# Five casts of wd, not three, between the last evacuation of gate and the search of blocks 1 to 3

## Chip, cores and metric

The kernel runs on one core of one Trainium2 chip. The metric is the device time of one launch in microseconds (us), lower is better. It is compared as the median of several runs; one more execution was taken with the hardware profiler, and all times inside the kernel are from that one.

## What is computed

The reference, for 2048 tokens x of width H = 1024, in float32, with I = 2752:

```python
s = silu(x @ w_gate.T)                       # 2048 x 2752
# in each row the I//2 entries of smallest |s| are set to 0
s = where_not_among_the_I//2_smallest_abs(s) * (x @ w_up.T)
x = layernorm(x + s @ w_down.T)
# second part: a feed forward layer with tiled quarter weights and rank-2 additions
g = silu(lin(x, w1q, a1, b1)) * lin(x, w3q, a3, b3)
x = layernorm(x + lin(g, w2q, a2, b2))       # lin = x @ tile(w,4).T + 0.5 * x @ A.T @ B.T
```

The change is in the first part: gate, the selection of the small entries, up and down (weights w_gate, w_up, w_down, in the kernel wg, wu, wd).

## The kernel before

The tokens are worked in four blocks of 512 (b = 0 to 3), each as four tiles t of 128 tokens. A matrix product in float32 precision is made of three passes of TensorE: each operand is split in a high part (a cast to fp32r) and a low part (the difference to the original), and `three` (lines 1405 to 1409) adds high x high, high x low and low x high.

**Pieces of weights.** All three weight matrices go through one ring of RING = 5 places in SBUF. A piece is 128 rows of the contraction by up to 512 columns, 256 KB. For each piece, in the same order everywhere:

- SyncE (SP) waits until TensorE has finished the piece five before it, whose place it takes (`load`, line 396, semaphore pe_used), and issues the load (line 398).
- ScalarE (ACT) casts it to its high part wh (`high_ring`, line 681).
- GpSimd (POOL) makes the low part wl (line 574).
- TensorE (PE) multiplies it with four tiles of tokens (lines 1407 to 1409): 12 matmuls of 512 columns for a piece.

Each engine does its pieces strictly in the order of the program. The order of TensorE is gate(0), up(0), and then for b = 1 to 3: gate(b) (48 pieces of wg), down(b-1) (44 pieces of wd, d = 0 to 43, called d0 to d43 here), up(b) (48 pieces of wu); at the end down(3). So the product with wd of a block runs between gate and up of the next one. The pieces d14 and d15 belong to the half-filled last chunk of rows; they take 8 matmuls, not 12 (lines 1498 and 1499).

**The search.** While TensorE is in down(b-1), VectorE (DVE) and ScalarE look for the threshold of each token of block b, in six rounds (called round 1 to 6). In a round VectorE writes a trial threshold (`negt`, line 969, semaphore probe) and counts the entries below it for tiles 0 and 1 (line 975, two passes); ScalarE counts for tiles 2 and 3 with four Sign activations (line 728), then raises the semaphore signs (line 735), for which VectorE waits (line 978) before it works out the next trial. Since ScalarE must go on casting weights, its search calls `piece()`, the cast of the next piece of wd, behind the first three Sign activations of each round, and 1 or 2 times more behind the round (line 824). A cast whose piece has not landed holds the Sign activation behind it.

After round 6 VectorE picks the exact threshold for the four tiles (lines 1021 to 1038); in front of the last pass of it, it takes the banks of PSUM with the sums of down(b-1), n = 0 (`take_down`, line 1125). The first matmuls of up(b) overwrite these banks and wait for that (line 1472, semaphore d_evac), tile by tile.

**Loads besides the weights.** Right behind the load of d28 SyncE issues the load of y, 2 MB of x in token order (lines 463 and 464), on the same queue.

Of the kernel before, what the change touches and what calls it, by code (L numbers as in the profile page):

```python
# [42 lines left out]
RING = 5  # L43
# [10 lines left out]
ND = 2 * NC  # L54
# [60 lines left out]
def down_at(b):  # L115
    return gate_at(b + 1) + (NG if b < NB - 1 else 0)
# [60 lines left out]
def program(nc, xT, xtok, wg, wu, wd, w13, w2, a13, a2, b1, b3, b2, out):  # L177
    x1 = nc.dram_tensor("x1", (NB, P, NT, H), F32, kind="Internal").ap()
    turning = nc.dram_tensor("turning", (NB, NJ, P, NT * CW), F32, kind="Internal").ap()
    with ExitStack() as ctx:  # L180
# [494 lines left out]
        def _(act):  # L675
# [7 lines left out]
            def high_ring(n, cols):  # L683
                high(raw_in[n % RING], 16 * (n // RING + 1), wh[:, ring(n, cols)], w_in_place[:, ring(n, cols)])
# [4 lines left out]
            def high_d(b, d):  # L689
                high_ring(down_at(b) + d, CW)  # L690
# [5 lines left out]
            def evac(b, j):  # L696

                for t in range(NT):
                    if t < NT - 1:
                        act.wait_ge(g_done, 3 * NJ * b + 3 * j + t + 1)  # L700
                    else:
                        act.wait_ge(pe_used, gate_at(b) + KH * (j + 1))
                    if b == 1:

                        act.wait_ge(u_freed, 8 + 4 * j + t + 1)
                    dst = s0[:, in_chunk(j, t)] if b == 0 else v[:, t, cols(j)]
                    nc.scalar.activation(dst, banks[2 * t + j % 2][:, 0:width(j)], ACT.Silu).then_inc(g_freed, 1)  # L707
# [13 lines left out]
            def search(b, piece, behind):  # L721

                for r in range(ROUNDS):
                    act.wait_ge(probe, ROUNDS * b + r + 1)
                    for t in (2, 3):
                        for h in range(2):
                            st.done()
                            ins = nc.scalar.activation(junka[:, :], v[:, t, h * (I // 2):(h + 1) * (I // 2)], ACT.Sign,  # L728
                                                       bias=negt[:, t:t + 1], accum_out=ssum[:, t - 2, h:h + 1])
                            st.mark(ins)  # L730
                            if t == 2 or h == 0:
                                piece()
                    st.done()

                    act.sem_inc(signs, 1)
                    for _ in range(behind[r]):
                        piece()

            def turned(b, n):

                for j, g in cast_at(b, n):
                    if g == 0:
                        act.wait_ge(t_in[j % 2], 16 * GROUPS * (NJ // 2 * b + j // 2 + 1))
                    nc.scalar.copy(h_part(hTh, j, g), h_part(landed, j, g)).then_inc(t_hi, 1)  # L744

            def up(b):

                for j in range(NJ):
                    for i in range(KH):
                        high_gu(up_at(b), KH * j + i)  # L750
                        turned(b, KH * j + i)
                    if j == 1:
                        norm(b - 1)
# [45 lines left out]
            ahead = iter(range(RING, NG))  # L799
# [16 lines left out]
            def down_then_up(b):  # L816

                for d in range(3):
                    high_d(b - 1, d)
                    if b == 1:  # L820
                        turned(0, NG + d)
                evac(b, NJ - 1)
                ahead = iter(range(3, ND))
                search(b, lambda: high_d(b - 1, next(ahead)), (1, 2, 2, 1, 1, 1))
                for d in ahead:
                    high_d(b - 1, d)
                up(b)

            gate_1()
            down_then_up(1)  # L830
            for b in range(2, NB):
                gate(b)
                down_then_up(b)
# [902 lines left out]
```

## Time and profile before

| | |
|---|---|
| time, median of 3 runs | 1923.15 us (1918.4 to 1924.95) |
| the profiled execution | 1917.84 us, span 1916.0 us |
| TensorE clock granted, mean | 0.999 of full |
| TensorE busy | 1886.9 us, 98% of the span |
| VectorE busy | 1338.0 us, 70% |
| ScalarE busy | 732.6 us, 38% |
| GpSimd busy | 935.7 us, 49% |

The span is from the first to the last instruction; 1.84 us lie around it. A row of the trace such as `378.14 0.50 PE L1407 ...` has the start in us from the beginning of the span, the duration in us, the engine, the line of the kernel and what is written from what; in brackets stands how long the engine was idle before it and who released it. Busy shares of TensorE come from pipelined matmuls with modelled ends, so starts are what is read below.

### The profile page before, as it was taken

How to read it: one execution, taken by the hardware profiler on the slowest of the kernel's cores; microseconds unless marked ns; L12 is line 12 of the kernel's file. 1: busy time of each engine (PE TensorE's matmuls, PEld its weight loads, DVE VectorE, ACT ScalarE, POOL GpSimd, SP SyncE). 2: the span in 40 equal slices, each digit the busy share in tenths (PEclk: the TensorE clock that was granted, in tenths of full speed). 3: DMA queues.
4: the chain of work that ended last, by engine and by line, in shares of the span. 5: the costliest groups of instructions: out<-in, count | busy, mean ns of one | idle time of the engine just before them, and what ended most of it. 6: DMA issues, size and time to landing. Idle time of an engine off the chain costs nothing. (4 is left out here: it accounts for less than half of the span.)

```text
span 1916.0 us, 24248 instructions
## 1 busy us (share of the span) xinstructions
PE 1886.9 (98%) x8952; PEld 1574.7 (82%) x8952; DVE 1338.0 (70%) x1958; ACT 732.6 (38%) x1192; POOL 935.7 (49%) x705
## 2 busy tenths in 40 slices
PE   9999999999999999999999999999999999999998
PEld 7898878888888898887878988889888777887776
DVE  2138898889877437897852489888218998469963
ACT  4347434563234336523243463233242332123312
POOL 5456895455556544555484455555581331013410
PEclk9999999999999999999999999999999999999999
DMA  4333348634478433436763334377742132212212
GB/s 148 91 102 95 99 148 229 177 100 139 125 227 246 114 87 103 145 98 213 192 199 95 96 101 138 121 237 208 221 145 77 57 117 91 88 43 70 97 44 88
DMA packets 119393, 249.78 MB, mean 130 GB/s; under 512 B 13412, under 2 KB 33892, under 8 KB 115920
## 3 DMA queue, kind: packets, MB, share of 16 engines
q1 hardware_dynamic: 114664, 231.43, 40.0%
q10 hardware_dynamic: 4608, 16.78, 2.2%
q8 instruction: 71, 1.16, 0.3%
q14 instruction: 50, 0.41, 0.1%
HBM read 208.31 MB, written 39.85 MB: 130 GB/s over the span
## 5 line engine op out<-in xcount | busy, mean ns | idle before, releaser
L574 POOL TENSOR_TENSOR wl<-w_in_place,wh 128x512 fp32r<-128x512 f32 (+2 forms) x552 | 736.9, 1342 | 600.0 <-ACT wh L681 598.5
L681 ACT CAST wh<-w_in_place 128x512 fp32r<-128x512 f32 (+2 forms) x560 | 328.3, 588 | 728.5 <-DMA w_in_place<-in_wg 283.1
L1407 PE MATMUL banks<-wh,xTh 128*128 128x512 f32 (+2 forms) x1536 | 566.2, 369 | 12.6 <-POOL wl L574 12.4
L1408 PE MATMUL banks<-wl,xTh 128*128 128x512 f32 (+2 forms) x1536 | 563.3, 367 | 0.0
L1409 PE MATMUL banks<-wh,xTl 128*128 128x512 f32 (+2 forms) x1536 | 563.2, 367 | 0.0
L1407 PEld LDWEIGHTS banks<-wh,xTh 128*128 128x128 f32 x1536 | 288.3, 188 | 61.7 <-POOL wl L574 21.7
L1409 PEld LDWEIGHTS banks<-wh,xTl 128*128 128x128 f32 x1536 | 288.3, 188 | 40.1
L1408 PEld LDWEIGHTS banks<-wl,xTh 128*128 128x128 f32 x1536 | 288.4, 188 | 39.6
L1407 PE MATMUL banks<-wh,hTh 128*128 128x512 f32 x672 | 262.2, 390 | 3.1 <-POOL wl L574 3.0
L1408 PE MATMUL banks<-wl,hTh 128*128 128x512 f32 x672 | 261.5, 389 | 0.0
L1409 PE MATMUL banks<-wh,hTl 128*128 128x512 f32 x672 | 261.5, 389 | 0.0
L728 ACT ACTIVATE junka<-v,negt 128x1376 int8<-128x1376 f32 x96 | 138.3, 1441 | 77.8 <-DVE negt L969 77.8
L1407 PEld LDWEIGHTS banks<-wh,hTh 128*128 128x128 f32 x672 | 126.1, 188 | 31.4 <-POOL wl L574 5.4
L975 DVE TENSOR_SCALAR_CACHE_REDUCE junkd<-v,tc 128x2752 int8<-128x2752 f32 x48 | 147.6, 3075 | 0.9
L1409 PEld LDWEIGHTS banks<-wh,hTl 128*128 128x128 f32 x672 | 126.1, 188 | 26.3
L1332 DVE SCALAR_TENSOR_TENSOR acc<-h,a2raw,acc 128x512 f32<-128x512 f32 (+1 forms) x168 | 146.5, 912 | 1.6
L1408 PEld LDWEIGHTS banks<-wl,hTh 128*128 128x128 f32 x672 | 126.1, 188 | 25.8
L1407 PE MATMUL banks<-xsh,w13h 128*128 128x512 f32 (+1 forms) x352 | 142.5, 405 | 0.0
L961 DVE TENSOR_SCALAR sgn<-v 128x512 int8<-128x512 f32 (+2 forms) x72 | 45.0, 625 | 138.6 <-ACT v L707 138.6
L1408 PE MATMUL banks<-xsl,w13h 128*128 128x512 f32 (+1 forms) x352 | 137.6, 391 | 0.0
L1409 PE MATMUL banks<-xsh,w13l 128*128 128x512 f32 (+1 forms) x352 | 137.4, 390 | 0.0
L1205 DVE TENSOR_TENSOR hTl<-landed,hTh 128x512 fp32r<-128x512 f32 (+1 forms) x96 | 104.9, 1136 | 45.4 <-ACT hTh L744 45.3
(143 smaller groups left out, 2176.1 us busy)
## 6 DMA issues: line engine op xcount, KB each, us to landing
w_in_place<-in_wd SPq DMA_DIRECT2D x176, 256.0 KB, 2.8
w_in_place<-in_wg SPq DMA_DIRECT2D x128, 256.0 KB, 2.7
w_in_place<-in_wu SPq DMA_DIRECT2D x128, 256.0 KB, 2.6
turning<-squares SPq DMA_DIRECT2D x16, 1024.0 KB, 4.9
landed<-turning SPq DMA_DIRECT2D x64, 256.0 KB, 5.5
w_in_place<-in_w SPq DMA_DIRECT2D x54, 256.0 KB, 2.9
x_in_place<-in_xT SPq DMA_DIRECT2D x32, 256.0 KB, 5.1
y<-in_xtok SPq DMA_DIRECT2D x4, 2048.0 KB, 7.8
```

The costliest lines, as they stand in the source:

```text
L574: nc.gpsimd.tensor_tensor(lo, landed, hi.bitcast(F32), ALU.subtract).then_inc(done, 1)
L681: nc.scalar.copy(hi, piece).then_inc(hi_done, 1)
L728: ins = nc.scalar.activation(junka[:, :], v[:, t, h * (I // 2):(h + 1) * (I // 2)], ACT.Sign, bias=negt[:, t:t + 1], accum_out=ssum[:, t - ...
L961: step(V.tensor_scalar(sgn[:, t, cols(j)], s, 0.0, 2.0, ALU.is_ge, ALU.mult))
L975: step(V.tensor_scalar(junkd[:, :], v[:, t, :], tc[:, 0, t:t + 1], None, ALU.is_lt, ALU.add, accum_out=tc[:, 1, t:t + 1]))
L1205: V.tensor_tensor(h_part(hTl, j, g), h_part(landed, j, g), h_part(hTh, j, g).bitcast(F32), ALU.subtract).then_inc(t_lo, 1)
L1332: step(V.scalar_tensor_tensor(out=part, in0=h2[0:rows, i, :], scalar=w, in1=part, op0=ALU.mult, op1=ALU.add))
L1407: nc.tensor.matmul(dst, ah, bh, start=start, stop=False)
L1408: nc.tensor.matmul(dst, ah, bl, start=False, stop=False)
L1409: return nc.tensor.matmul(dst, al, bh, start=False, stop=stop)
```

## The change

```diff
@@ down_then_up(b) of ScalarE, line 816
                 evac(b, NJ - 1)
-                ahead = iter(range(3, ND))
+                for d in range(3, RING):
+                    high_d(b - 1, d)
+                ahead = iter(range(RING, ND))
                 search(b, lambda: high_d(b - 1, next(ahead)), (1, 2, 2, 1, 1, 1))
                 for d in ahead:
                     high_d(b - 1, d)
```

Before, ScalarE cast d0, d1 and d2, evacuated the last chunk of gate and entered the search; d3 was cast behind the first Sign activation. Now d3 and d4 are cast before the search, and each place in the search has a piece two later than it had. The number of casts in the search stays 26. What the other engines do, and in which order, is unchanged.

ScalarE where the search of block 1 begins. Names: v is what the search counts in, banks are PSUM, wh is the high part of a piece and w_in_place the landed piece; raw_in0 to raw_in4 are the semaphores of the five places of the ring (d3 waits for raw_in2, d4 for raw_in3). Before:

```order
L707 ACTIVATE v<-banks 128x320 [waits u_freed,pe_used]
L728 ACTIVATE junka,ssum<-v,negt 128x1376 [waits act_s,probe]
L681 CAST wh<-w_in_place 128x512 [waits raw_in2]
L728 ACTIVATE junka,ssum<-v,negt 128x1376 [waits act_s]
L681 CAST wh<-w_in_place 128x512 [waits raw_in3]
```

Now, in the same place:

```order
L707 ACTIVATE v<-banks 128x320 [waits u_freed,pe_used]
L681 CAST wh<-w_in_place 128x512 [waits raw_in2]
L681 CAST wh<-w_in_place 128x512 [waits raw_in3]
L728 ACTIVATE junka,ssum<-v,negt 128x1376 [waits act_s,probe]
L681 CAST wh<-w_in_place 128x512 [waits raw_in4]
```

The casts of d3 (raw_in2) and d4 (raw_in3) moved ahead of the first Sign activation, and d5 (raw_in4) follows it.

ScalarE in round 6, the last, of the search of block 1; the row that waits for probe begins the round. Before, with d25 (raw_in4), d26, d27 between the Sign activations and d28 (raw_in2), d29 (raw_in3) behind them:

```order
L728 ACTIVATE junka,ssum<-v,negt 128x1376 [waits act_s,probe]
L681 CAST wh<-w_in_place 128x512 [waits raw_in4]
L728 ACTIVATE junka,ssum<-v,negt 128x1376 [waits act_s]
L681 CAST wh<-w_in_place 128x512 [waits raw_in0]
L728 ACTIVATE junka,ssum<-v,negt 128x1376 [waits act_s]
L681 CAST wh<-w_in_place 128x512 [waits raw_in1]
L728 ACTIVATE junka,ssum<-v,negt 128x1376 [waits act_s]
L681 CAST wh<-w_in_place 128x512 [waits act_s,raw_in2]
L681 CAST wh<-w_in_place 128x512 [waits raw_in3]
```

Now, with d27 (raw_in1), d28, d29 (raw_in3) between them and d30 (raw_in4) behind:

```order
L728 ACTIVATE junka,ssum<-v,negt 128x1376 [waits act_s,probe]
L681 CAST wh<-w_in_place 128x512 [waits raw_in1]
L728 ACTIVATE junka,ssum<-v,negt 128x1376 [waits act_s]
L681 CAST wh<-w_in_place 128x512 [waits raw_in2]
L728 ACTIVATE junka,ssum<-v,negt 128x1376 [waits act_s]
L681 CAST wh<-w_in_place 128x512 [waits raw_in3]
L728 ACTIVATE junka,ssum<-v,negt 128x1376 [waits act_s]
L681 CAST wh<-w_in_place 128x512 [waits act_s,raw_in4]
```

The cast of d29 moved from behind the round to a place ahead of its fourth Sign activation.

## Rows read from the trace of the kernel before

**Rows 1.** The page, part 1: busy time of each engine.

```profile
PE 1886.9 (98%) x8952; PEld 1574.7 (82%) x8952; DVE 1338.0 (70%) x1958; ACT 732.6 (38%) x1192; POOL 935.7 (49%) x705
```

**Rows 2.** Groups by line, TensorE: busy us, mean ns, idle before, releaser.

```profile
L1407 PE MATMUL banks<-wh,hTh 128*128 128x512 f32 x672 | 262.2, 390 | 3.1 <-POOL wl L574 3.0
```

**Rows 3.** Timeline, block 1, first matmul of d3 on TensorE.

```profile
378.14 0.50 PE L1407 MATMUL banks<-wh,hTh 128*128 128x512 f32 x1 [2.11 <-POOL wl L574]
```

**Rows 4.** Timelines of ScalarE and GpSimd, block 1, round 1: first Sign, d3.

```profile
374.70 1.44 ACT L728 ACTIVATE junka<-v,negt 128x1376 int8<-128x1376 f32 x1 [4.84 <-DVE negt L969]
376.14 0.60 ACT L681 CAST wh<-w_in_place 128x512 fp32r<-128x512 f32 x1
...
376.82 1.27 POOL L574 TENSOR_TENSOR wl<-w_in_place,wh 128x512 fp32r<-128x512 f32 x1 [6.39 <-ACT wh L681]
```

**Rows 5.** Timeline of SyncE, block 1: issues of d7, d28, y and d29.

```profile
376.13 0.33 SPq L398 DMA_DIRECT2D w_in_place<-in_wd  x1
...
434.06 0.33 SPq L398 DMA_DIRECT2D w_in_place<-in_wd  x1
434.50 0.37 SPq L455 DMA_DIRECT2D y<-in_xtok  x1
...
436.78 0.33 SPq L398 DMA_DIRECT2D w_in_place<-in_wd  x1
```

**Rows 6.** The same, block 2 and then block 3: d7 and d29 of each.

```profile
734.98 0.33 SPq L398 DMA_DIRECT2D w_in_place<-in_wd  x1
...
793.89 0.33 SPq L398 DMA_DIRECT2D w_in_place<-in_wd  x1
...
1096.42 0.33 SPq L398 DMA_DIRECT2D w_in_place<-in_wd  x1
...
1155.61 0.33 SPq L398 DMA_DIRECT2D w_in_place<-in_wd  x1
```

**Rows 7.** One tile's view, loads of wd in 366 to 434 us.

```profile
DMA to landing us min/median/max: 2.6/2.7/3.0
```

**Rows 8.** DMA issues, KB and us to landing: y of block 1; d29 of blocks 1, 2, 3.

```profile
y<-in_xtok SPq DMA_DIRECT2D x1, 2048.0 KB, 7.9
...
w_in_place<-in_wd SPq DMA_DIRECT2D x1, 256.0 KB, 6.3
...
w_in_place<-in_wd SPq DMA_DIRECT2D x1, 256.0 KB, 6.1
...
w_in_place<-in_wd SPq DMA_DIRECT2D x1, 256.0 KB, 7.0
```

**Rows 9.** One tile's view, all six loads of y in the kernel.

```profile
DMA to landing us min/median/max: 7.6/8.3/9.7
```

**Rows 10.** Waits of VectorE, 370 to 440 us: total, times, longest.

```profile
DVE sadd L979 <- ACTq L735: 8.7, 6, 1.5
```

**Rows 11.** Timeline of ScalarE: fourth Sign of round 6, blocks 1, 2, 3.

```profile
437.89 1.44 ACT L728 ACTIVATE junka<-v,negt 128x1376 int8<-128x1376 f32 x1
...
795.00 1.44 ACT L728 ACTIVATE junka<-v,negt 128x1376 int8<-128x1376 f32 x1
...
1156.73 1.44 ACT L728 ACTIVATE junka<-v,negt 128x1376 int8<-128x1376 f32 x1
```

**Rows 12.** Timeline of VectorE: take_down, n = 0, blocks 1, 2, 3.

```profile
485.18 2.48 DVE L1125 TENSOR_TENSOR y<-banks,y 128x512 f32<-128x512 f32 x4
...
842.02 2.48 DVE L1125 TENSOR_TENSOR y<-banks,y 128x512 f32<-128x512 f32 x4
...
1202.58 2.63 DVE L1125 TENSOR_TENSOR y<-banks,y 128x512 f32<-128x512 f32 x4 [1.49 <-PE banks L1409]
```

**Rows 13.** Groups by line, VectorE: take_down in the whole kernel.

```profile
L1125 DVE TENSOR_TENSOR y<-banks,y 128x512 f32<-128x512 f32 x32 | 20.3, 681 | 33.7 <-PE banks L1409 33.6
```

**Rows 14.** Timeline of TensorE: first matmul of up(1), up(2), up(3).

```profile
488.20 0.39 PE L1407 MATMUL banks<-wh,xTh 128*128 128x512 f32 x1
...
845.31 0.39 PE L1407 MATMUL banks<-wh,xTh 128*128 128x512 f32 x1
...
1207.03 0.39 PE L1407 MATMUL banks<-wh,xTh 128*128 128x512 f32 x1
```

## The prediction

> **What bounds the kernel now.** I read the page first: TensorE is busy for 98% of the span [rows 1], at a granted clock of 0.999, which is its upper level of 2.4 GHz, in every slice. So only what starts or stops TensorE can move the time, and the change touches ScalarE alone. Next I read the groups by line, for what TensorE waits for inside down: over 672 first matmuls of the pieces of wd it waited 3.0 us in all, for the low parts that GpSimd makes [rows 2]. The timeline shows where most of it lies: 2.11 us at d3 of block 1 [rows 3]. The chain behind it is in the timelines of ScalarE and GpSimd [rows 4]: ScalarE had been idle for 4.84 us, waiting for the first trial threshold, ran the first Sign at 374.70, cast d3 only at 376.14, GpSimd took 1.27 us from 376.82, and TensorE started 0.05 us behind its end. This is what the change removes. The reader is to see also that ScalarE was idle in front of that Sign, so that casts there cost nothing.
>
> Then I followed the search itself, because two pieces more are now cast inside its timed part, and it ends in something that TensorE waits for. In each of the six rounds VectorE waits for ScalarE's signs, 8.7 us in all and 1.5 at the longest [rows 10]. So ScalarE is the slower half of every round, and a delay of a Sign goes straight into the length of the search.
>
> **The gain on TensorE.** Every load waits for the end of the piece five before it, so the issues on SyncE show TensorE's pace: d28 to d29 is 2.72 us [rows 5], 12 matmuls of 0.227. From the issue of d7 to that of d29 are 22 steps; undisturbed they take 22 x 2.72 = 59.84 us, less 2 x 0.91 for d14 and d15 with 8 matmuls each, that is 58.02. The rows say 60.65 in block 1 [rows 5], 58.91 and 59.19 in blocks 2 and 3 [rows 6]. The excess, 2.63, 0.89 and 1.17 us, is all that TensorE lost in this stretch, 4.69 us together. It is more than the 3.0 of the groups, because a stop also costs a slower first matmul and the small stops are not all listed; I take the issues. I credit it in full, since d3 and d4 will be cast in the idle stretch: d7 was issued at 376.13, so d4, three pieces earlier, at about 368, and with the usual 2.7 us [rows 7] it landed near 371, well before 374.70 [rows 4]. In blocks 2 and 3 the first trial comes a little earlier against the loads, but by the same counting back d4 lands near 729.5 and 1091.0, some 2 us ahead of it (an estimate), so the start of the search is not delayed (a small delay would be swallowed below anyway).
>
> **The cost in the search.** Every place in the search now casts a piece that lands two pieces, 5.4 us, later. A piece can be cast no sooner than 2.7 us behind the end of the piece five before it. Counting landings by 2.72 us against the places of the casts, I find the places in rounds 1 to 5 just met, or missed by under 1 us, at most about 2 us in sum in one block (an estimate). In round 6 it is otherwise. There the third cast, ahead of the fourth Sign, is now d29. d29 is the piece issued behind the 2 MB load of y [rows 5], and it took 6.3, 6.1 and 7.0 us to land in the three blocks [rows 8], not 2.7. y took 7.9 us from 434.50, thus to 442.4, and d29 landed at 436.78 + 6.3 = 443.1, right behind it. Before, d29 was cast after the search, where this harmed nobody. Its landing is a point in time, so what the earlier rounds lose is swallowed by it and not added.
>
> The Trainium skill, page "DMA: Bandwidth & Descriptors", section "Queues, rings and completion order", says that on each DMA engine the descriptors of a queue are consumed in ring order, though a later one may finish its write first. The rows agree in that d29 did not overtake y; by the second half of the sentence it could, and the sum would then be that of the first rival below.
>
> The fourth Sign of round 6 starts, at the earliest, 0.60 us (the cast, [rows 4]) behind the landing. With TensorE and so the loads earlier by the gain:
>
> Block 1: 436.78 - 2.63 + 6.3 + 0.6 = 441.05, against 437.89 [rows 11]: 3.16 us later.
> Block 2: 793.89 - 0.89 + 6.1 + 0.6 = 799.70, against 795.00: 4.70 us later.
> Block 3: 1155.61 - 1.17 + 7.0 + 0.6 = 1162.04, against 1156.73: 5.31 us later.
>
> **What waits for the search.** Behind the last signs VectorE has an unbroken stretch of picking up to take_down, which it reached at 485.18, 842.02 and 1202.58 - 1.49 = 1201.09 [rows 12]. In blocks 1 and 2 it did not idle there: TensorE had finished the banks already. The first tile of take_down takes 0.68 us [rows 13], and TensorE can follow 0.05 us behind as it did behind GpSimd (together 0.73). TensorE began up at 488.20, 845.31 and 1207.03 [rows 14]; so the cover over VectorE's chain was 488.20 - 485.91 = 2.29, 2.56 and 5.21 us. That is the cover that hides the change's cost, and the gain on TensorE eats it too. New starts of up:
>
> Block 1: TensorE ready at 488.20 - 2.63 = 485.57, VectorE at 485.18 + 3.16 + 0.73 = 489.07. The later decides: +0.87 us against before.
> Block 2: ready at 844.42; VectorE at 842.02 + 4.70 + 0.73 = 847.45: +2.14.
> Block 3: ready at 1205.86; VectorE at 1201.09 + 5.31 + 0.73 = 1207.13: +0.10.
>
> TensorE's four tiles of the first piece of up are 3 x 0.227 = 0.68 us apart and VectorE's are 0.62 (2.48 for four, [rows 12]), so only the first tile waits. The blocks add, since each search starts from its own block's gate. Sum: +3.1 us. Nothing given back later is counted: VectorE's later work in up is shifted with TensorE, and the second half of take_down is needed only after 8 pieces, 21.8 us, of up. In block 0's search and in the last down nothing changed, and no instruction was added or removed.
>
> Against the profiled execution, 1917.84, this is 1921.0 us; the median of the runs shown is 5.3 us above that execution, and put on the median it is **1926.3 us**. About 0.3%, 5.8 us, is what a measurement of this kernel can tell from no change.
>
> **Rivals.**
>
> First, the gain stays. If d29 landed in the usual 2.7 us, the fourth Sign would not be delayed in block 1 (landing at 436.9, its cast's place before 437.3), by 1.3 us in block 2 and 1.0 in block 3. Up would start at 485.91, 844.42 and 1205.86: -2.29, -0.89, -1.17, together -4.3 us, 1918.8 on the median. Against it speak all three rows of d29 [rows 8]; for it only that y's data might travel otherwise in another run. Even this is within 0.3%. The Trainium skill, page "Perfetto Trace Analysis", section "Optimization Strategy", advises to find the gaps on the limiting engine and make what they wait for start sooner. The change does just that, and by this rule alone the sum would be the whole -4.7 us; the rows of round 6 are why I do not follow it.
>
> Second, slower by more than 0.3%: y takes its longest. Loads of y took 7.6 to 9.7 us [rows 9]. If all three took 9.7 and d29 moved with them (y of block 1 took 7.9; I take 1.8 us more there, 2.0 in block 2, 1.0 in block 3, estimates from the spread), the sum is 3.1 + 4.8 = +7.9 us, 1931.1. It decides from 0.9 us more in each block. Since these rows come from one execution and a landing varies with what else is read, this has some weight.
>
> Third, the change doesn't do what it says: TensorE still stops at d3 and its companions for another reason, such as the low part of the tokens. Then the loads are not earlier, and d29 is late in full: the Sign starts at 443.68, 800.59 and 1163.21, up at 491.70, 848.34 and 1208.30: +3.5, +3.0, +1.3, together +7.8 us. The rows name GpSimd's low part as the releaser [rows 3], which speaks against it.
>
> **How the numbers follow.** The forecast (up starts held by VectorE in blocks 1 and 2, sum between +1 and +6 us, 1924 to 1929 by itself) has 0.68; the first rival 0.13; the second 0.11; the third 0.04; other 0.04. The median of the runs itself wanders by some 3 us. The range from the first rival to the second, 1919 to 1931, leaves out less than 2 in 10. Slower by over 0.3% takes the second and third and a small part of the forecast pushed by the spread of the runs: 0.18. Faster by over 0.3% would need the first rival and luck: 0.04. Within: 0.78.
>
> **What the new profile would show.** The wait of 2.11 us at d3 gone, and the group of first matmuls on wd waiting near 0 for GpSimd. d7 to d29 on SyncE near 58.0 us. A new wait of ScalarE's cast in round 6 for the load of wd, some 3 us in block 1 and 4 to 5 in blocks 2 and 3, and VectorE waiting in round 6 by as much more than 1.5 us for the signs. A new wait of TensorE for VectorE's y (line 1125) at the start of up: 3.5, 3.0 and 1.3 us. If the waits at d3 go and TensorE does not wait for VectorE, the first rival holds. If waits of the casts already pile up in rounds 2 to 5 beyond 2 us, my counting of the landings was wrong. What would make the prediction wrong in sign is a d29 that lands early.

## The result, and the profile after

The changed kernel takes 1933.99 us, the median of six runs (1931.87 to 1935.95); the kernel before takes 1922.28 us, the median of six (1918.4 to 1924.95). The ratio on record is 1.0076, with a 95% interval of 1.0064 to 1.0087: slower by about 14.6 us. The two medians as they stand are only 11.7 us apart, a ratio of 1.0061 and just below that interval, and the record does not say how its ratio was weighed; so the loss is known as 12 to 15 us and not closer. The forecast was 1926.3 us and its range ended at 1931. The profiled execution of the changed kernel has a span of 1934.2 us and a time of 1935.95 us, its slowest run, and the one of before was that kernel's fastest, so the two spans differ by 18.2 us. In the page, TensorE's busy time grew from 1886.9 [rows 1] with the same number of instructions:

```profile
PE 1892.4 (98%) x8952; PEld 1580.5 (82%) x8952; DVE 1349.5 (70%) x1958; ACT 732.1 (38%) x1192; POOL 933.5 (48%) x705
```

That already tells something: 5.5 us more of the same matmuls means that some of them ran slower.

**Down has lost its stops.** The groups by line show no wait at all at the first matmuls of wd, where there were 3.0 us [rows 2]. In up a wait is new, put down to "issue", which means that the profile shows nothing that the engine waited for:

```profile
L1409 PE MATMUL banks<-wh,xTh 128*128 128x512 f32 (+2 forms) x1536 | 568.8, 370 | 27.7 <-POOL wl L574 14.6 <-issue 13.0
...
L1409 PE MATMUL banks<-wh,hTh 128*128 128x512 f32 x672 | 261.4, 389 | 0.0
```

SyncE's timeline gives d7 and d29 of block 1, 58.03 us apart, where they were 60.65 apart [rows 5]. In blocks 2 and 3 the distance is 58.02 too, where it was 58.91 and 59.19 [rows 6].

```profile
377.97 0.33 SPq L398 DMA_DIRECT2D w_in_place<-in_wd  x1
...
436.00 0.33 SPq L398 DMA_DIRECT2D w_in_place<-in_wd  x1
```

**The search ends later.** The view of transfers gives d29's time to land in the three blocks, which was 6.3, 6.1 and 7.0 [rows 8]:

```profile
w_in_place<-in_wd SPq DMA_DIRECT2D x1, 256.0 KB, 6.4
...
w_in_place<-in_wd SPq DMA_DIRECT2D x1, 256.0 KB, 6.0
...
w_in_place<-in_wd SPq DMA_DIRECT2D x1, 256.0 KB, 7.6
```

ScalarE's timeline shows its cast in round 6 waiting for that load, in each block, with the fourth Sign (of block 1 here) right behind:

```profile
442.39 0.62 ACT L681 CAST wh<-w_in_place 128x512 fp32r<-128x512 f32 x1 [1.25 <-DMA w_in_place<-in_wd]
442.92 1.44 ACT L728 ACTIVATE junka<-v,negt 128x1376 int8<-128x1376 f32 x1
...
804.91 0.62 ACT L681 CAST wh<-w_in_place 128x512 fp32r<-128x512 f32 x1 [1.87 <-DMA w_in_place<-in_wd]
...
1172.61 0.62 ACT L681 CAST wh<-w_in_place 128x512 fp32r<-128x512 f32 x1 [4.28 <-DMA w_in_place<-in_wd]
```

The waits of 1.25 and 1.87 us are smaller than the 3 and 4 to 5 that the prediction named for blocks 1 and 2, because the search reached round 6 late already; the 4.28 of block 3 is as it said. VectorE waits for the signs of round 6 2.8, 3.4 and 5.8 us, where it had been 1.5. And the casts of rounds 2 to 5 wait for their own loads: 0.9, 2.9 and 4.3 us in sum in the three blocks, where it had been 0.2. The prediction had allowed about 2 us in a block and had named more than that as a sign that its counting of the landings was wrong; in blocks 2 and 3 it was.

**TensorE stops at the start of up.** Its timeline, with the last matmul of down(1) first, then the first of up(1), up(2) and up(3):

```profile
487.19 0.39 PE L1411 MATMUL banks<-wh,hTl 128*128 128x512 f32 x1
491.39 0.53 PE L1409 MATMUL banks<-wh,xTh 128*128 128x512 f32 x1 [3.81 <-issue]
491.72 0.63 PE L1410 MATMUL banks<-wl,xTh 128*128 128x512 f32 x1
...
494.71 0.57 PE L1411 MATMUL banks<-wh,xTl 128*128 128x512 f32 x1
495.11 0.39 PE L1409 MATMUL banks<-wh,xTh 128*128 128x512 f32 x1
...
854.28 0.76 PE L1409 MATMUL banks<-wh,xTh 128*128 128x512 f32 x1 [3.78 <-issue]
...
1221.98 0.76 PE L1409 MATMUL banks<-wh,xTh 128*128 128x512 f32 x1 [5.38 <-issue]
```

"Issue" names no releaser, but VectorE's timeline does. Its first tile of take_down starts 0.79 us ahead of each of these matmuls; the prediction had taken 0.73:

```profile
490.60 2.48 DVE L1127 TENSOR_TENSOR y<-banks,y 128x512 f32<-128x512 f32 x4
...
853.49 2.48 DVE L1127 TENSOR_TENSOR y<-banks,y 128x512 f32<-128x512 f32 x4
...
1221.19 2.49 DVE L1127 TENSOR_TENSOR y<-banks,y 128x512 f32<-128x512 f32 x4
```

**And then it runs at half clock.** The matmuls behind the first stop take 0.63 us instead of 0.39 and start 0.43 us apart instead of 0.227. The windows (length, TensorE's busy time and matmuls, granted clock, DMA) say why: 0.50 is TensorE's lower level, 1.2 GHz.

```profile
485.00:490.00 5.00, 2.58 (x12) 1.00 0.36 105
490.00:495.00 5.00, 3.61 (x9) 0.67 0.00 0
855.00:860.00 5.00, 5.00 (x14) 0.50 0.00 0
1220.00:1225.00 5.00, 3.02 (x7) 0.50 0.00 0
```

In the kernel before, the first matmul of each up took 0.39 us [rows 14], and there was no stop.

The next table follows each block from the start of its down (the first matmul on hTh): S1 is the first Sign of the search, S4 the fourth Sign of round 6, "down out" VectorE's start of take_down, "up" TensorE's first matmul of up, all in us from that start. "Stop" is TensorE's idle time ahead of up, from the last matmul's regular end. "Half clock" counts the matmuls at the lower level behind it and what they cost beside 0.227 us each.

| kernel, block | S1 | S4 | down out | up | stop | half clock |
|---|---|---|---|---|---|---|
| before, 1 | 7.08 | 70.27 | 117.56 | 120.58 | 0 | 0 |
| before, 2 | 5.31 | 68.47 | 115.49 | 118.78 | 0 | 0 |
| before, 3 | 5.38 | 68.75 | 114.60 | 119.05 | 0 | 0 |
| after, 1 | 9.03 | 73.39 | 121.07 | 121.86 | 3.97 | 8, 1.69 us |
| after, 2 | 7.68 | 72.99 | 121.04 | 121.83 | 3.93 | 14, 2.92 us |
| after, 3 | 7.45 | 74.58 | 122.64 | 123.43 | 5.53 | 8, 1.78 us |

It accounts for most of the 18.2 us between the two spans. Up starts later by 1.28, 3.05 and 4.38 us, together 8.71; half clock costs 6.39. Another 1.91 us arose ahead of the first down of block 1, where nothing was changed (367.62 against 369.53), and is taken as the spread of the runs. 1.2 us are left over. The two executions are the slowest and the fastest of their kernels, so this explains one pair of them, not the difference of the medians to a microsecond.

### The profile page after: what moved, and what is told of

Its sections match the earlier page's. It is cut to its first block and busy times, and to the rows that moved or that the text cites. A ratio compares the mean times of both kernels' runs of the same rounds, so it can differ in the third digit from the quotient of the medians.

```text
span 1934.2 us, 24248 instructions
## 1 busy us (share of the span) xinstructions
PE 1892.4 (98%) x8952; PEld 1580.5 (82%) x8952; DVE 1349.5 (70%) x1958; ACT 732.1 (38%) x1192; POOL 933.5 (48%) x705
## 3 DMA queue, kind: packets, MB, share of 16 engines
q8 instruction: 71, 1.16, 0.3%
## 5 line engine op out<-in xcount | busy, mean ns | idle before, releaser
L1409 PE MATMUL banks<-wh,xTh 128*128 128x512 f32 (+2 forms) x1536 | 568.8, 370 | 27.7 <-POOL wl L574 14.6
L963 DVE TENSOR_SCALAR sgn<-v 128x512 int8<-128x512 f32 (+2 forms) x72 | 50.2, 697 | 138.2 <-ACT v L707 138.2
L1207 DVE TENSOR_TENSOR hTl<-landed,hTh 128x512 fp32r<-128x512 f32 (+1 forms) x96 | 100.9, 1095 | 43.4 <-ACT hTh L744 43.1
```

Source lines behind the costliest of these rows:

```text
L963: step(V.tensor_scalar(sgn[:, t, cols(j)], s, 0.0, 2.0, ALU.is_ge, ALU.mult))
L1207: V.tensor_tensor(h_part(hTl, j, g), h_part(landed, j, g), h_part(hTh, j, g).bitcast(F32), ALU.subtract).then_inc(t_lo, 1)
L1409: nc.tensor.matmul(dst, ah, bh, start=start, stop=False)
```

## The experiments

All ratios are the recorded ones, against the kernel before run on the same chip; the quotient of the two medians can lie up to 0.15% from them. Runs with different edits were partly made on different chips, so two of these kernels are compared by their ratios. "From the profile" sums two things of one profiled execution: how much later than before its ups start relative to their downs, and the half-clock cost behind that start. What happens later in up is not in it.

| kernel | median us (runs) | ratio [95%] | stops ahead of up 1, 2, 3 | from the profile |
|---|---|---|---|---|
| the change | 1933.99 (6) | 1.0076 [1.0064, 1.0087] | 3.97, 3.93, 5.53 | 8.7 + 6.4 |
| change, y late | 1924.08 (12) | 1.0023 [1.0011, 1.0035] | 0.23, 0, 0.42 | -4.1 |
| before, y late | 1922.55 (11) | 1.0007 [0.9997, 1.0016] | 0, 0, 0 | +1.6 |
| four ahead | 1915.10 (10) | 0.998 [0.9971, 0.9989] | 0, 0, 0 | -4.3 |
| five ahead, two given back | 1918.66 (11) | 0.9995 [0.9986, 1.0003] | 0, 0, 0 | -2.2 |
| before, one pass more | 1929.97 (6) | 1.0049 [1.0031, 1.0067] | 0, 0.69, 1.51 | +3.2 |
| before, two passes more | 1938.18 (6) | 1.0091 [1.0071, 1.0112] | 4.17, 3.72, 0.96 | 8.4 + 5.1 |
| change, GpSimd held | 1933.35 (5) | 1.0086 [1.0072, 1.0101] | 4.01, 3.82, 4.02 | 7.5 + 7.1 |
| four ahead, one given back | 1918.88 (12) | 1.0005 [0.9996, 1.0015] | 0, 0, 0 | +0.3 |
| change, y late, GpSimd held | 1919.91 (12) | 1.0002 [0.999, 1.0014] | 0, 0.40, 0 | -3.9 |
| change, y late, norm late | 1917.64 (12) | 0.999 [0.9979, 1.0001] | 3.01, 0, 0.22 | -1.5 + 1.5 |
| four ahead, norm late | 1914.86 (11) | 0.9975 [0.9965, 0.9985] | 0.39, 0, 0 | -3.3 |

### Is it d29 behind y?

The load of y is issued six pieces later, so that no piece cast in round 6 lies behind it. The same edit is made to the kernel before, as a control:

```diff
-                    if d == 28:
+                    if d == 34:
                         x_tiles(b - 1)
```

> The changed kernel, with the 2 MB load of y issued behind d34 and not behind d28. My theory now: the loss has three parts, (A) VectorE's first trial of the search comes some 2 us later because GpSimd makes the low parts of d3 and d4 while VectorE works on the last chunk of gate, (B) the landing of d29 behind y holds the fourth Sign of round 6, and (C) TensorE's stop at the start of up, 3.8 to 5.4 us, is followed by 1.7 to 2.9 us of matmuls at half clock. Without y in front, d29 lands in 2.7 us and B is gone: the idle before its cast in round 6 falls to 0, the stops at up shrink to under 2.5 us and no clock drop follows. Time within 4 us of the kernel before, some 10 us under the changed kernel. Rival (the casts come too late in all rounds, whatever y does): it stays at least 8 us slower than before.

> Control: the kernel before with y issued behind d34. Both theories: no change, within 2 us of before, since d29 was cast behind the search and y is needed only at take_down.

With the change, the edit takes the ratio from 1.0076 to 1.0023, and the stops from 4 to 5.5 us to 0.42 at most. The view of transfers gives d29 of block 1, and then d35, which now stands behind y:

```profile
w_in_place<-in_wd SPq DMA_DIRECT2D x1, 256.0 KB, 2.8
...
w_in_place<-in_wd SPq DMA_DIRECT2D x1, 256.0 KB, 6.3
```

No cast of round 6 waits for its load any more, and the fourth Sign of block 1 falls back from 73.39 to 71.12. It is still 0.8, 1.6 and 2.3 us later than before in the three blocks: the casts of rounds 2 to 5 still wait for their loads, 2.2, 4.4 and 3.0 us in sum. The control stays where it was, 1.0007, so moving y does nothing by itself. d29 behind y is the largest single cause. But the expectation that nothing of the loss would be left failed: the ups start 4.1 us earlier than before in sum, and the kernel is still slower by 0.23%. Something else costs some 8 us; the run of the norm below takes that up.

### Is it the number of casts ahead?

Four pieces ahead of the search, so that each place casts only one piece later than before; and five ahead with two taken out of rounds 1 and 2, so that the places in rounds 3 to 6 cast what they did before:

```diff
-                ahead = iter(range(3, ND))
+                for d in range(3, RING - 1):
+                    high_d(b - 1, d)
+                ahead = iter(range(RING - 1, ND))
```

```diff
-                search(b, lambda: high_d(b - 1, next(ahead)), (1, 2, 2, 1, 1, 1))
+                search(b, lambda: high_d(b - 1, next(ahead)), (0, 1, 2, 1, 1, 1))
```

> Only d3, not d3 and d4, is cast ahead of the search, y where it was. The third cast of round 6 is then d28, which is issued ahead of y. Theory: B is gone, A is halved (one low part of GpSimd beside VectorE, first trial about 1 us later), the wait at d3 is gone: up starts about 1 us earlier in each block, time 1 to 4 us under before. Rival (what costs is that GpSimd and ScalarE work there at all, or late landings in all rounds): 3 us or more slower than before.

> Five ahead as in the change, but one cast fewer behind round 1 and behind round 2, so that from round 3 on every place casts the piece that it had before. Theory: A stays (first trial 2 us later), B is gone, no stop over 1.5 us at up, no clock drop: 0 to 3 us under before. If A alone were the cause of the loss, it would be as slow as the changed kernel, 10 us or more over before.

Four ahead is faster than before: 0.998 [0.9971, 0.9989], 3.8 us. Its ups start 2.21, 0.88 and 1.16 us earlier, 4.25 in sum, which is all but 0.44 of the 4.69 us that TensorE lost in down. So the gain that the prediction worked out is there to be had. In this kernel the third cast of round 6 is d28, issued ahead of y. Giving two back ties with before, 0.9995 [0.9986, 1.0003]; its fourth Signs are back at 70.37, 68.54 and 68.92, those of before within 0.2 us, though S1 is still 2 us late. That also speaks for d29: the same five casts ahead harm nobody as long as d29 is cast after the search. It cannot tell d29 from the late casts of the early rounds, though, since the waits of those are gone as well; the run with y late can.

### What does a stop at the start of up cost?

Here no cast is moved. VectorE alone gets one or two more counting passes over a tile behind the search, ahead of take_down (extra work that changes no result):

```diff
                     if b and t == NT - 1:
+                        for _ in range(2):
+                            step(V.tensor_scalar(junkd[:, :], v[:, t, :], tc[:, 0, t:t + 1], None, ALU.is_lt, ALU.add,
+                                                 accum_out=tc[:, 1, t:t + 1]))
+                            st.done()
                         take_down(b - 1, 0)
```

> The kernel before, no cast moved; VectorE makes one pass more over tile 3 (line 975's operation, 3.08 us, its result overwritten later by the same value) ahead of take_down, n = 0, in the searches of blocks 1 to 3. Theory: the cover of 2.3, 2.6 and 5.2 us takes most of it, TensorE stops 0.8, 0.5 and 0 us at up, the clock stays up, time 1 to 3 us over before. Rival (any stop there costs clock): drops at half clock, 5 us or more.

> The same with two passes more, 6.16 us. Theory: TensorE stops 3.9, 3.6 and 1 us at up, as long as in the changed kernel for blocks 1 and 2, and is at half clock for 1.7 to 2.9 us worth of delay behind the first two stops, none behind the third: time 12 to 15 us over before. Rival (the half clock of the changed kernel has another cause than the stop): no half clock, 8.5 us over before.

Two passes give stops of 4.17, 3.72 and 0.96 us. The timeline of TensorE and the windows behind the three stops:

```profile
492.73 0.77 PE L1411 MATMUL banks<-wh,xTh 128*128 128x512 f32 x1 [4.01 <-issue]
```

```profile
495.00:500.00 5.00, 5.00 (x18) 0.72 0.11 32
860.00:865.00 5.00, 5.00 (x17) 0.70 0.18 49
1225.00:1230.00 5.00, 5.00 (x24) 1.00 0.37 104
```

Half clock follows the two stops of about 4 us and not the one of 0.96, in a kernel in which nothing of the change was made. It costs 2.45 and 2.64 us there, some two thirds of the stop itself. The kernel came out slower than the 12 to 15 us expected of it: 17.5 us by the ratio. Its profile has half clock at two more places, around 1270 and 1854 us, which the expectation had not counted. With one pass the stops of 0.69 and 1.51 us are followed by the full clock. So a stop of some 4 us, wherever it comes from, brings the half clock; this is shown.

Shorter stops do not decide alone. The kernel before stops for 2.11 us at d3 of block 1 [rows 3] and keeps its clock; the control with y late stops for 2.12 us at the same place and loses it. The windows of the kernel before come first, then those of the control:

```profile
380.00:385.00 5.00, 5.00 (x24) 1.00 0.18 55
```

```profile
380.00:385.00 5.00, 5.00 (x17) 0.70 0.00 0
```

The kernel with one pass stops for 1.79 us there and loses it as well. What decides at that length stays open; that it is a part of the spread of this kernel's runs is likely but not shown. One pass was also slower than was expected of it: 1.0049 where its ups explain 3.2 us. Its profile has half clock at two more places and waits of 2.3 and 2.2 us for norm in up (see below), which the expectation had not counted.

### Why is the first trial late?

S1 comes about 2 us later than before in all blocks, though d4 landed in time as predicted. The timelines of VectorE and GpSimd, at the end of block 2's gate:

```profile
734.80 1.40 DVE L963 TENSOR_SCALAR sgn<-v 128x320 int8<-128x320 f32 x1
736.24 0.49 DVE L965 SCALAR_TENSOR_TENSOR v<-v 128x320 f32<-128x320 f32 x1
...
736.66 1.41 DVE L963 TENSOR_SCALAR sgn<-v 128x320 int8<-128x320 f32 x1
...
738.52 0.32 DVE L963 TENSOR_SCALAR sgn<-v 128x320 int8<-128x320 f32 x1
```

```profile
734.70 1.32 POOL L574 TENSOR_TENSOR wl<-w_in_place,wh 128x512 fp32r<-128x512 f32 x1 [0.53 <-ACT wh L681]
736.25 1.63 POOL L574 TENSOR_TENSOR wl<-w_in_place,wh 128x512 fp32r<-128x512 f32 x1 [0.22 <-ACT wh L681]
```

The same operation takes 0.32 us alone and 1.40 when it starts 0.10 us behind GpSimd's; both of the long ones end 0.2 us behind the end of GpSimd's. The earlier casts of d3 and d4 let GpSimd make the low parts just then. The Trainium skill, page "SBUF — State Buffer", section "SBUF: two separate sides", says that VectorE and GpSimd share a pair of ports under an exclusive lock, for which the later of the two waits out the other's whole instruction. It says so of VectorE operations in a 2-port performance mode or with two inputs in SBUF; whether this one, with a single input, runs in such a mode, no run here shows. The rows agree in that VectorE's operation ends just behind GpSimd's, and where GpSimd started second, at 736.25, its own took 1.63 instead of 1.32.

To test it, GpSimd is held at d3 until the first trial is out:

```diff
                 s = ring(n)
+                if d == 3 and b < NB - 1:
+                    pool.wait_ge(probe, ROUNDS * (b + 1) + 1)
```

> The changed kernel, but GpSimd waits with the low part of d3 (and so of d4) until VectorE has written the first trial of the search. Theory: VectorE's last chunk of gate is undisturbed again, first Sign at 7.1, 5.3 and 5.4 us behind the start of down as in the kernel before, not 9.0, 7.7 and 7.5; the landing of d29 still holds round 6 where it is the later one, so 1 to 6 us under the changed kernel. Rival (GpSimd has no part in it, ScalarE's casts delay the first trial): first Sign as late as in the changed kernel.

The first Sign is back at 7.06, 5.38 and 5.34, where it was before, so this cause of the late S1 is shown. VectorE's timeline of this kernel, in block 1, has the short form ahead of the first trial:

```profile
373.25 0.32 DVE L965 TENSOR_SCALAR sgn<-v 128x320 int8<-128x320 f32 x1
```

The time, though, did not move: 1.0086 [1.0072, 1.0101] beside 1.0076, where less was expected. The casts wait the longer for their loads instead: those of rounds 1 to 5 for 6.8, 9.4 and 9.4 us in sum in the three blocks instead of 0.9, 2.9 and 4.3, that of d29 for 3.03 us in block 1 instead of 1.25. S4 is no earlier in blocks 1 and 2 (73.77 and 73.28) and 1.1 us earlier in block 3 (73.51):

```profile
442.61 0.62 ACT L683 CAST wh<-w_in_place 128x512 fp32r<-128x512 f32 x1 [3.03 <-DMA w_in_place<-in_wd]
```

Do these 2 us count with y out of the way?

> The changed kernel with both cures, y issued behind d34 and GpSimd held with the low part of d3 until the first trial. Theory: first Sign at 7.1, 5.4 and 5.3 us behind the start of down, fourth Sign of round 6 about 1 us behind the kernel before (waits for landings only), the stop at d3 gone: 1 to 4 us under before, 5 us or more under the version with y late alone. Rival (the low parts made beside VectorE do not matter to the time): as slow as the version with y late alone, 4 us over before.

1.0002 [0.999, 1.0014] against 1.0023 [1.0011, 1.0035] for y late alone: some 4 us less, though the two intervals just overlap, and short of what was expected (under before, and 5 us under y late alone). Where the 4 us come from is not shown. S1 is back at 7.07, 5.47 and 5.28, but the ups start 3.9 us earlier than before in sum, and with y late alone it was 4.1; the casts of rounds 1 to 5 wait for their loads for 6.8, 9.3 and 9.5 us in sum. So these loads swallow the earlier first trial, with y and without it.

### Between the two best

Four ahead and one given back combines the edits above:

> Only d3 ahead, and no cast behind round 1, so that from round 2 on every place casts the piece that it had before. Theory: as the version with four ahead, 2 to 6 us under before; if waits for landings in rounds 2 to 6 cost that version anything, this one is the faster of the two. Rival (four ahead gained by something else than the wait at d3): no faster than before.

This missed: 1.0005 [0.9996, 1.0015], worse than four ahead alone. With no cast behind round 1, the first piece of round 2 is late, and TensorE waits for GpSimd in down again, 2.1 us in block 1 and 0.9 in each of the others. The places in the early rounds are not slack; they are what keeps down fed.

### What still costs with y late?

In up, ScalarE's norm waits for VectorE's nbias, and behind it in ScalarE's program stand casts of wu. Timelines of ScalarE, before, then the change, then the change with y late:

```profile
524.82 1.24 ACT L764 ACTIVATE y<-y,nbias,rstd 128x1024 f32<-128x1024 f32 x1 [3.01 <-DVE nbias L1146]
```

```profile
530.74 1.24 ACT L764 ACTIVATE y<-y,nbias,rstd 128x1024 f32<-128x1024 f32 x1 [4.00 <-DVE nbias L1148]
```

```profile
525.09 1.24 ACT L764 ACTIVATE y<-y,nbias,rstd 128x1024 f32<-128x1024 f32 x1 [5.36 <-DVE nbias L1148]
```

VectorE's statistics are the end of its long chain from the search. In the kernel before, VectorE started take_down 3.0 us ahead of TensorE's first matmul of up; in the other two it is only 0.8 us ahead. So norm starts 36.6 us behind the start of up before, 39.4 in the change and 38.8 with y late. In the change the half clock holds TensorE back too; with y late it doesn't, and the casts run out. TensorE's timeline of the kernel with y late:

```profile
532.53 0.50 PE L1409 MATMUL banks<-wh,xTh 128*128 128x512 f32 x1 [2.46 <-POOL wl L574]
```

In that stretch of up, TensorE waited 0.3 us in the kernel before and 1.2 in the change; in block 3 of the kernel with y late it waited 2.3. So the norm is put one chunk later:

```diff
-                    if j == 1:
+                    if j == 2:
                         norm(b - 1)
```

> The version with y late alone, but ScalarE's norm of the rows of y (line 764) one chunk of up later, behind the third and not the second. Theory: in that version VectorE reaches nbias late against TensorE, ScalarE waits for it with the casts of the third chunk behind, and TensorE stops 2.5 us twice; with norm a chunk later these stops are gone and the time falls by 3 to 6 us, to within 2 us of before. Rival (its loss lies in the search): it stays 4 us over before.

> Four ahead with the norm a chunk later, looked for as the best version. Theory: there TensorE still waits some 2 us in sum in up where the casts stand behind norm; 4 to 8 us under before. Rival (the later store of x1 makes VectorE or the loads of the next chunk wait): no faster than four ahead alone, or slower.

The change with y late and norm late comes to 0.999 [0.9979, 1.0001], from 1.0023 without the second edit: 6.3 us. In block 1 TensorE no longer waits in that stretch (525 to 550), where it had waited 2.5, and in block 3 it waits 0.1 instead of 2.3. So the waits were norm's. What norm late would do to the kernel before was not run. Four ahead with norm late is 0.9975 [0.9965, 0.9985], 4.8 us faster than before and the best of all; its lead over four ahead alone lies inside the intervals. Its row of first matmuls on wd in blocks 1 to 3, with 0.6 us of waits left:

```profile
L1409 PE MATMUL banks<-wh,hTh 128*128 128x512 f32 x504 | 196.3, 389 | 0.6 <-POOL wl L574 0.6
```

## Why the prediction was wrong

**Right: the gain on TensorE.** 4.69 us were predicted; the issues are now 58.03 and twice 58.02 us apart instead of the 58.02 worked out, and four ahead realises 4.25 of it.

**Right: the delay of the fourth Sign.** Predicted 3.16, 4.70 and 5.31 us; measured from the start of down, 3.12, 4.52 and 5.83. That it came out so near has a reason: the fourth Sign hangs on the landing of d29, whatever the rounds before it lose. With GpSimd held, the first trial was 2 us earlier, and the fourth Sign was not in blocks 1 and 2. The losses of the early rounds were larger than counted, as the waits of the casts show (up to 4.3 us in a block), and with y late they are what keeps the fourth Sign 0.8 to 2.3 us late.

**Wrong as put, without effect here: "the start of the search is not delayed".** It was, by 1.95, 2.37 and 2.07 us. The counting of loads was right, but casts earlier on ScalarE also mean low parts earlier on GpSimd, and these met VectorE's last operations of the gate. It is swallowed by the landings that the casts wait for, in the change and with y late as well.

**Mis-sized: the new starts of up.** The sum was to be +3.1 us (0.87, 2.14, 0.10) and was 8.71 (1.28, 3.05, 4.38). The step that failed is that the delay of the fourth Sign was added to take_down's old start, as if VectorE's stretch between them kept, block by block, the length that it had in one execution. It was 47.29, 47.02 and 44.36 us before and 47.68, 48.05 and 48.06 after. In block 3 that made 3.70 of the 4.28 us of error: 44.36 is the shortest such stretch of the thirteen profiled kernels in any block, and the prediction read its cover of 5.21 us as belonging to the kernel when it belonged to that execution. Laid side by side, instruction by instruction, the stretches of block 3 show where the 3.70 us went. VectorE's timeline, first before, then with the change:

```profile
1160.50 0.17 DVE L1004 TENSOR_TENSOR hc<-hc,qa 128x8 f32<-128x8 f32 x1
...
1160.98 1.65 DVE L1024 SCALAR_TENSOR_TENSOR scr<-v,hc 128x1376 f32<-128x1376 f32 x1
...
1176.90 1.15 DVE L1006 TENSOR_TENSOR hc<-hc,qa 128x8 f32<-128x8 f32 x1
...
1178.17 1.15 DVE L1021 TENSOR_SCALAR qa<-hc 128x4 f32<-128x4 f32 x1
1179.35 2.73 DVE L1026 SCALAR_TENSOR_TENSOR scr<-v,hc 128x1376 f32<-128x1376 f32 x1
...
1187.61 1.21 DVE L1033 SCALAR_TENSOR_TENSOR pick<-iota,qa,top 128x8 f32<-128x8 f32 x1
```

These four took 0.17, 0.17, 1.65 and 0.33 us before: 3.92 us more, and three others took 0.2 less. Each of the four starts within 0.2 us of the start of a subtraction of GpSimd; the three short ones end 0.02 to 0.03 us behind its end. GpSimd did four pieces in a row just then, where before it had been idle from 1160.36 to 1163.34:

```profile
1175.48 5.16 POOL L574 TENSOR_TENSOR wl<-w_in_place,wh 128x512 fp32r<-128x512 f32 x4 [0.88 <-ACT wh L681]
...
1187.50 1.30 POOL L574 TENSOR_TENSOR wl<-w_in_place,wh 128x512 fp32r<-128x512 f32 x1 [0.84 <-ACT wh L681]
```

So the cover of 5.21 us belonged to a stretch that met few such collisions, and in block 3 the mis-sized term is made of them. They do not need the change: the kernel before with y late casts d29 where it always was, and its stretch of block 3 is 48.06 us too. Which instructions meet was nothing that the prediction could count; its error was to take the shortest of three stretches as given.

**Missing: the clock.** The prediction counted a stop at its length. Three stops of 3.93 to 5.53 us brought matmuls at 1.2 GHz worth 6.39 us more. The term was nowhere in the sum, and it is the largest single error. Together with the one above (5.6 us) it makes 12.0 us; the forecast of +3.1 us becomes +15.1. The ratio says 14.6, the medians 11.7 and the two profiled spans 18.2, so the sum has the right size, and that it meets the first of the three so closely is luck.

**Wrong: "Nothing given back later is counted".** Norm in ScalarE's program ties up's casts to VectorE's statistics. In the change this costs little, 1.2 us of waits in block 1, since the stop has already delayed TensorE. Where the stop is gone it takes back the gain and more: 6.3 us by the run with y late and norm late. The prediction looked at VectorE's later work alone and did not ask who waits for it through a third engine.

Of the rivals, the one on the slower side named the right place, a start of up held by a late d29, but explained it by a longer load of y. d29's landing of 6.4, 6.0 and 7.6 us was almost what it had been. The bound decided earlier, by the two errors above.

## What to carry to other kernels

Before moving a load's consumer forward, find the transfer that it now waits for and what stands ahead of it in its queue. A buffer of slack that one execution shows at one place (here 5.21 us in block 3 beside 2.29 and 2.56) should be taken at the smallest of its kind. And a stop of the limiting engine should be priced with what follows it, and the engine that was helped followed on to the next place where it meets the one that was delayed.

## What the runs showed of the hardware

- Stops of TensorE of 3.0 to 5.5 us were always followed by the lower clock level, for 7 to 14 matmuls and 1.5 to 2.9 us of loss: nine stops in four kernels. Of the stops ahead of up, none of 1.51 us or less was. Elsewhere it went either way: waits of 2.11, 2.31 and 2.46 us kept the clock, 1.47, 1.79, 2.12, 2.27 and 2.49 did not.
- A VectorE operation of 0.32 us takes 1.40 when GpSimd's subtraction of 1.32 us has just started, one of 0.17 us over 8 elements takes 1.15, and VectorE's 1.65 us operation over 1376 elements takes up to 2.8. Its MAX8 over 1376 elements took 1.59 to 1.60 us and its counting pass 3.07 to 3.08 in all thirteen profiles, whatever GpSimd did.
- A load of 256 KB issued behind one of 2 MB on the same queue lands in 6.0 to 7.6 us instead of 2.7 [rows 7], in blocks 1 to 3 of both kernels; with y issued later, the same load takes 2.6 to 2.8.
